# A graph network kernel whose head-layer pass goes from eight chunks of 13 edge groups to nine, the last two of 8 and 5, and stores its segment ends chunk by chunk

## What is computed

```python
k, q, v = typed_linear(x, ntype, Wk / Wq / Wv)      # each reshaped to (N, H, Dh)
a = einsum('eho,eho->eh', k[src] @ rel_att, q[dst]) * rel_pri / sqrt(Dh)
m = einsum('ehd,hdo->eho', v[src], rel_msg)
ae = exp(a - segment_max(a, dst)[dst])
attn = ae / segment_sum(ae, dst)[dst]
h_agg = segment_sum(m * attn[..., None], dst)       # a sum over the edges of each node
```

## Time and profile before

| | |
|---|---|
| Time, median of 3 runs | 3181.16 us (3181.05 to 3183.84) |
| Time of the profiled execution | 3180.5 us |
| its span | 3178.7 us |
| `head_pass` in the span, first gather to last `add` | 1564.2 to 2180.5 us |
| PE / DVE / ACT / POOL busy, share of the span | 65% / 52% / 27% / 64% |
| PE's granted clock, mean of the span | 0.633 |

### The profile page before, as it was taken

The page is one execution under the profiler, slowest core; times in us unless marked ns, Lnnn a source line. Parts: engine busy times, 40 slices in busy tenths (PEclk is TensorE's granted clock), DMA queues, the critical chain, the costliest instruction groups (busy, mean ns, idle before and its releaser), DMA issues. The chain is left out here.

```text
span 3178.7 us, 42733 instructions
## 1 busy us (share of the span) xinstructions
PE 2068.4 (65%) x10207; PEld 1789.9 (56%) x10207; DVE 1638.1 (52%) x5183; ACT 869.5 (27%) x2627; POOL 2021.1 (64%) x1758
## 2 busy tenths in 40 slices
PE   5458888887676998999437777774445555554530
PEld 2347777776565877787336666663444444444430
DVE  3367777776212344333346666666754444444436
ACT  2356666664022443343100000000022222222210
POOL 3477766750006777776277777741568888888883
PEclk8655555555557999999655555555666666666665
DMA  6655544440504333333244444430055555555545
GB/s 223 226 148 145 148 135 134 136 120 2 209 17 103 91 96 84 98 96 83 65 129 134 136 135 134 134 94 10 17 96 77 81 79 78 81 79 78 80 49 186
DMA packets 311499, 337.21 MB, mean 106 GB/s; under 512 B 113362, under 2 KB 229391, under 8 KB 309977
## 3 DMA queue, kind: packets, MB, share of 16 engines
q0 software_dynamic: 113152, 163.68, 24.9%
q1 hardware_dynamic: 198138, 171.17, 17.5%
HBM read 260.56 MB, written 75.68 MB: 106 GB/s over the span
## 5 line engine op out<-in xcount | busy, mean ns | idle before, releaser
L2396 POOL DMA_INDIRECT side<-e_merged,e_row x416 | 649.3, 1561 | 142.7 <-issue 114.6
L1323 POOL DMA_INDIRECT e_gathered<-msg_src_table,src_idx x416 | 405.6, 975 | 276.8 <-POOLq L368 150.3
L673 POOL DMA_INDIRECT e_gathered<-rel_src_table,rel_idx x416 | 435.5, 1047 | 204.0 <-issue 122.5
L1740 POOL DMA_INDIRECT e_kv<-kv_table,e_idx x416 | 422.7, 1016 | 126.0 <-issue 125.2
L2306 PE MATMUL e_ps_t<-ident,e_onehot 128*128 128x128 f32 x104 | 46.3, 447 | 389.4 <-DVE e_onehot L1233 389.4
L1787 PE MATMUL e_ps_q<-e_window,e_spread 64*128 64x128 f32 x832 | 214.8, 437 | 111.5 <-DMA e_window<-q_table 68.7
L730 PE MATMUL e_ps_a<-e_typed,e_rel 128*128 128x72 f32 x832 | 206.0, 429 | 98.8 <-DVE e_typed L854 98.8
L716 PE MATMUL e_ps_r<-e_window,e_spread 64*128 64x128 f32 x832 | 215.3, 437 | 66.6 <-DMA e_window<-rel_dst_table 37.8
L1787 PEld LDWEIGHTS e_ps_q<-e_window,e_spread 64*128 64x128 f32 x832 | 185.1, 325 | 127.3 <-DMA e_window<-q_table 94.0
L730 PEld LDWEIGHTS e_ps_a<-e_typed,e_rel 128*128 128x128 f32 x832 | 185.1, 328 | 122.8 <-DVE e_typed L854 102.3
L2306 PEld LDWEIGHTS e_ps_t<-ident,e_onehot 128*128 128x128 f32 x104 | 18.1, 174 | 416.4 <-DVE e_onehot L1233 416.4
(11 more groups left out here) (419 smaller groups left out, 4263.1 us busy)
## 6 DMA issues: line engine op xcount, KB each, us to landing
e_src_all<-src_padded SPq DMA_DIRECT2D x104, 256.0 KB
e_keys<-tile_keys SPq DMA_DIRECT2D x104, 128.0 KB
e_window<-rel_dst_table SPq DMA_DIRECT2D x416, 32.0 KB
e_offsets<-group_offsets SPq DMA_DIRECT2D x104, 128.0 KB
e_mixed<-in_edge_attr_dram SPq DMA_DIRECT2D x103, 128.0 KB
rel_src_table<-t_up SPq DMA_DIRECT2D x5, 2560.0 KB, 9.0
n_parts<-side SPq DMA_DIRECT2D x40, 320.0 KB
side<-n_zeros SPq DMA_DIRECT2D x48, 256.0 KB
```

The costliest lines, as they stand in the source:

```text
L673: pool.indirect_dma_start(gathered[:, q % GS, j, :], None, rel_table, bass.IndirectOffsetOnAxis(ap=rel_idx[:, q * J + j:q * J + j + 1], ax ...
L1323: pool.indirect_dma_start(gathered[:, q % GS, j, :], None, msg_table, bass.IndirectOffsetOnAxis(ap=src_idx[:, q * J + j:q * J + j + 1], ax ...
L1740: pool.indirect_dma_start(kv[:, slot, j, :], None, kv_table, bass.IndirectOffsetOnAxis(ap=idx[:, half, k * J + j:k * J + j + 1], axis=0)). ...
L2396: pool.indirect_dma_start(side[copy], bass.IndirectOffsetOnAxis(ap=row[:, s4, j:j + 1], axis=0), merged[:, s4, j, :], None, compute_op=ALU ...
```

## The change

The chunk sizes become a list, [13, 13, 13, 13, 13, 13, 13, 8, 5]; `AT[c]` is the first group of chunk c and `PARTS` is 9. Loops of DVE, PE, ACT and SP run over PARTS, with a test that leaves out what a short chunk doesn't have. A softening still works on all 104 rows; of a short chunk only 8 or 5 rows of each head are meant. SP stores the ends of chunk c - 1 (8 DMAs) ahead of `links(c)`, and of the last chunk at the end. POOL takes the indices straight from `src_idx`, without copies and their waits, with a no-op before each group. The DVE part of the diff, left out but for one piece, does the same with the loop's indices.

```diff
-            idx = tmp("idx", [P, 2, CH * J], I32)
+            SIZES = [CH] * (NCH - 1) + [8, 5]
+            AT = [sum(SIZES[:c]) for c in range(len(SIZES) + 1)]
+            PARTS = len(SIZES)
+            chunk_of = [(c, i) for c in range(PARTS) for i in range(SIZES[c])]
...
-            row_ends = tmp("row_ends", [ROWS, NCH, 4])
+            row_ends = tmp("row_ends", [ROWS, PARTS, 4])
...
-                stage(0, 0)
-                for c in range(NCH):
-                    chunk(c, c % 2)
+                for q in range(Q):
+                    hold(pool, weighed, q - RING + 1)
+                    pool.nop(nofuse=True)
+                    for j in range(J):
+                        pool.indirect_dma_start(kv[:, q % RING, j, :], None, kv_table,
+                                                bass.IndirectOffsetOnAxis(ap=src_idx[:, q * J + j:q * J + j + 1], axis=0)).then_inc(src_in[q % RING], 16)
...
-                        sp.dma_start(pen_c[h * CH:(h + 1) * CH, :], pen_row[c * CH:(c + 1) * CH, :]).then_inc(links_in, 16)
+                        sp.dma_start(pen_c[h * CH:h * CH + SIZES[c], :], pen_row[AT[c]:AT[c + 1], :]).then_inc(links_in, 16)
...
+                def store_ends(c):
+                    sp.wait_ge(soft, SOFT * (c + 1))
+                    for h in range(H):
+                        sp.dma_start(head_ends[AT[c]:AT[c + 1], h, :], row_ends[h * CH:h * CH + SIZES[c], c, :]).then_inc(ends_st, 16)
...
-                for c in range(NCH):
+                for c in range(PARTS):
+                    if c > 0:
+                        store_ends(c - 1)
                     links(c)
-                    for k in range(CH):
-                        load(CH * c + k)
-                sp.wait_ge(soft, SOFT * NCH)
-                for h in range(H):
-                    sp.dma_start(head_ends.rearrange("(c i) h n -> i c h n", i=CH)[:, :, h, :], row_ends[h * CH:(h + 1) * CH, :, :]).then_inc(ends_st, 16)
-                sp.wait_ge(ends_st, 16 * H)
+                    for k in range(SIZES[c]):
+                        load(AT[c] + k)
+                store_ends(PARTS - 1)
+                sp.wait_ge(ends_st, 16 * H * PARTS)
...
-                for c in range(NCH + 1):
+                for c in range(PARTS + 1):
                     for k in range(CH):
-                        if c < NCH:
-                            expand(CH * c + k)
-                        if c > 0:
-                            total_up(CH * (c - 1) + k)
-                    if c < NCH:
+                        if c < PARTS and k < SIZES[c]:
+                            expand(AT[c] + k)
+                        if c > 0 and k < SIZES[c - 1]:
+                            total_up(AT[c - 1] + k)
+                    if c < PARTS:
                         soften(c)
...
-                            if c < NCH and k > 0:
+                            if expanding and k > 0:
                                 score(q - 1)
-                    if c < NCH:
-                        if nw == 1:
-                            score(CH * c + CH - 1)
+                            if c < PARTS and k == SIZES[c] - 1:
+                                score(q)
+                    if c < PARTS:
                         soften(c)
```

More of the change, by code:

```diff
@@ L1720, in head_pass @@
             cleared, ends_st, ends_in = sem("cleared"), sem("ends_st"), sem("ends_in")
-            staged, win_in, offsets_in = pair("staged"), pair("win_in"), pair("offsets_in")
+            win_in, offsets_in = pair("win_in"), pair("offsets_in")
             src_in = pair("src_in", RING)
@@ L1803, in soften @@
                 def soften(c):
-                    pe.wait_ge(reduced, CH * (c + 1))
+                    pe.wait_ge(reduced, AT[c + 1])
                     for j in range(J):
@@ L1844, in score @@
                 def score(q):
-                    c, i = divmod(q, CH)
+                    c, i = chunk_of[q]
                     dve.wait_ge(expanded, nw * (q + 1))
@@ L1865, in weigh @@
                 def weigh(p):
-                    c, i = divmod(p, CH)
+                    c, i = chunk_of[p]
                     dve.wait_ge(attn_ready, c + 1)
@@ L1906, in soften @@
                     dve.tensor_tensor(ex[:, :], ex[:, :], run[:, :], ALU.mult).then_inc(soft, 1)
-                for c in range(NCH + 1):
+                for c in range(PARTS + 1):
                     for k in range(CH):
-                        q, p = CH * c + k, CH * (c - 1) + k
-                        if c < NCH:
+                        expanding = c < PARTS and k < SIZES[c]
+                        totalling = c > 0 and k < SIZES[c - 1]
+                        q, p = AT[min(c, PARTS - 1)] + k, AT[c - 1] + k if c else 0
+                        if expanding:
                             for w in range(nw):
                                 spread_out(q, w)
-                        if c > 0:
+                        if totalling:
                             weigh(p)
                         if nw > 1:
-                            if c > 0:
+                            if totalling:
                                 add(p)
-                            if c < NCH:
+                            if expanding:
                                 score(q)
                         else:
-                            if c > 0:
+                            if totalling:
                                 mark(p, 0)
```

2 lines of the change are left out of this document (1 added, 1 removed).

## The result

The changed kernel takes 3228.8 us (median of 4 runs, 3228.1 to 3229.8), the kernel before beside it 3181.1 us (4 runs). The ratio is 1.0151 [1.0134, 1.0169]: it is slower by 47.7 us, where +50.0 was forecast. The profiled execution has a span of 3226.3 us at a mean granted clock of 0.631 (before: 3178.7 at 0.633).

What follows compares the result with a forecast made beforehand. SP's issue time between chunks was taken to be on the path of the whole pass. The terms 2.2 + 22.2 + 26.4 - 0.8 gave +50.0 us on 3180.5, so 3230.5 us; range 3212 to 3246.

Steps and rivals of the forecast that it cites:

- the signs that were named: Changed profile: eight waits of about 13.4 us, chunks 76.2 us apart, pairs 3.90 us, clock 0.50, no wait for `ends`.
- Term 1: PE's lone totals: 13 before and after, so no tail gain; new bubble of 1.1 us at two places, +2.2 us.
- Term 2: One more place between chunks, with softening, 16 links and first loads: +22.2 us, bounds 21 and 23.
- The bound of 21: Added place between chunks: lower bound in us if links of 5 rows issue as fast as the shortest store.
- Term 3: SP's queue between chunks: eight stores ahead of the links at eight places, 3.3 us each, +26.4 us.
- the rival with dearer places: Places between chunks: 24 DMAs in a burst land later or stores issue at 0.5 us; +64, 3245 us; chance 0.07.
- Term 4: End of the pass: five lone totals cover the last stores and the load of `ends`; nothing added.
- Term 5: POOL, mostly start and chunk 0: copies go, no-op taken as free; -0.8 us.
- Hidden stores: SP between chunks: the stores' issue is hidden or nearly free; +23.6, 3204 us; chance 0.06.
- Lone totals with cover in the middle: Short turns: lone totals find cover, so the tail's gain of 13.8 us is real; 3214.5 us; chance 0.03.
- A faster clock: PE in the pass: the new order lifts its clock from 0.50 to full speed; 3167 us; chance 0.04.

Runs made afterwards that it cites:

- the first experiment: Kernel before, eight chunks, with the eight stores of each chunk's ends ahead of the next chunk's links; first 3852.4 us (1.0064), repeated 3203.9 us (1.0080).

## Why the prediction was right

**What bounds the kernel.** SP's issue time between chunks is on the path: shown from three sides, by adding DMAs (13.9 and 16.8 us a place), by moving them back (10.2) and by taking the wait away (0). Of the signs that were named, eight waits, the pair of 3.90 us, the clock of 0.50, the last gather at 2111 us and no wait for `ends` came as said; the waits between chunks of 13 were 14.2 us and not 13.4, and those chunks 77.2 us apart and not 76.2.

**Term 1, the split of the totals, +2.2.** The main point holds: 13 lone totals before and after, so the short tail is no gain. The bubble was 2 x 0.6 = 1.2 us, half of what was forecast, but the bursts of lone totals are 0.8 us longer in three pieces than in one, so the term comes to 2.0.

**Term 2, one place more, +22.2.** The kernel with the stores behind the loads has terms 1, 2 and 5 in it; it came to +21.6 us by its median and +24.1 by the pass, where 23.6 was forecast. The bound of 21 that the prediction kept for short links was the right thought: two places had them, at 0.34 us a link in place of 0.41, 1.1 us off each. The prediction saw the short links only at the new place.

**Term 3, eight stores at eight places, +26.4.** The changed kernel against the one with the stores behind: 3228.8 - 3200.7 = 28.1 us, 3.5 a place. The two were not measured side by side; taken each against the kernel before beside it, the difference is 26.0, by the waits it is 109.2 - 81.3 = 27.9 and by the passes 29.4. The issue was sized right (3.24 against 3.3 us at a place of 13 rows). What was left out is the landing, 0.8 us later in the mean at six of the eight places of the changed kernel; what delays it stays open. Of the rival with dearer places this one half happened: it had allowed a microsecond for it. The rule of the Trainium skill ("DMA: Bandwidth & Descriptors", Issuing engines are not separate DMA queues), by which the time to start a DMA is usually small beside the DMA, would have given 3204: one such DMA is indeed short here, 0.4 us against the offsets' landing of 2.7 to 3.9, but 16 or 24 of them in a row are not.

**Term 4, the end of the pass, nothing.** Held, no wait for `ends`.

**Term 5, POOL, -0.8.** Too small for the measurement to show or to exclude (0.9999 [0.9990, 1.0008]). In the traces it isn't seen: the first gather starts 0.12 us after SP's first link before and 0.08 us after it in the changed kernel.

**The rivals.** Hidden stores: refuted by two experiments. Lone totals with cover in the middle: the tail did fall by 13.6 us, and the two turns ahead of it took it back. A faster clock: 0.50 in every stretch of the pass, also in the changed kernel. The forecast and the result differ by 1.7 us, but that is closer than the working deserves: the pass itself grew by 53.5 us, 3.5 more than the sum, and 5.0 us of the layers ahead, which vary from run to run, stood against it.

## What to carry to other kernels

At a point where all engines wait for one another, a queue's issue time is time of the kernel: count the DMAs between the semaphore and the first load that somebody waits for, put loads that need nothing of that semaphore ahead of it (36 us here, against the kernel before), stores last, and merge what can be one DMA (24.8 us became 3.0, in the kernel of eight chunks). Splitting the last chunk to shorten a tail moves lone work into other turns where one engine paces both, and brings the fixed cost of a chunk with it. When the largest wait goes, work out the next bound first: half of the 10 us at each place was given to POOL's gathers.

## What the runs showed of the hardware that was not expected

A link's issue on SP took 0.29 us for 5 or 8 rows and 0.37 for 13, and a store of 104 rows of 16 bytes took 0.34. The time from the offsets' issue to the `spread_out` that waits doesn't follow the number of DMAs ahead of them. It was 2.7 to 2.9 us behind 16 in the kernel before and 2.9 to 3.3 behind 16 in the kernel with the stores behind the loads. Behind 24 it was 3.0 to 3.4 with the stores alone, and in the changed kernel 3.4 to 3.9 at six places and 2.8 at two; behind 32 it was 2.8 to 3.5. What sets it no run here shows.

The kernel before took 3825 us (3798 to 3842 in 18 runs) on one chip and 3181, 3179 and 3178 where it was measured otherwise. The gathers' own durations were nearly the same: these are the page's groups of gathers of the first experiment's kernel there (busy, mean ns | idle before):

```profile
L2401 POOL DMA_INDIRECT side<-e_merged,e_row x416 | 650.2, 1563 | 142.7 <-issue 104.5 <-DMA side<-e_merged,e_row 21.6 <-ACT e_merged L2333 16.5
L1740 POOL DMA_INDIRECT e_kv<-kv_table,e_idx x416 | 418.9, 1007 | 377.7 <-DVE e_weighted L1874 256.7 <-issue 120.6 <-POOL e_idx L1732 0.4
```

POOL's 1007 ns a gather in the head pass are the 1016 of the earlier trace rows, but 256.7 us of waits for DVE have been added; in `propagate`, the one pass that is written as a loop of the chip and not unrolled, the idle time is 142.7 us, to the tenth what it is in the profile of the kernel before. In the head pass DVE stood still for up to 14 us at a time where the profile names no engine:

```profile
2152.80 0.16 DVE L1889 COPY parts<-e_ps_a 128x2 f32<-128x2 f32 x1 [14.11 <-remote]
```

Why this chip stretches the unrolled passes and not the looped one no run here tests; it stays open. The waits at the places came out much the same there (10.1 us without stores, 13.3 with the stores ahead, 9.7 behind, 16.2 doubled; the first eight stores brought 3.2 us, their issue alone), so the mechanism could be read from those runs, but not the 0.6% of the POOL part.
